# Attention masks on TensorE: two heads' mask matmuls as four quarters of the array, with key tiles taken in swapped pairs by every second head

## The chip, the cores and the metric

The kernel runs on one core of a Trainium2 chip. The metric is the device time of one execution in microseconds (us); lower is better. TensorE multiplies with an array of 128 rows by 128 columns that can also be used in parts (32 or 64 rows or columns each), VectorE and ScalarE read its results from PSUM, GpSimd does some elementwise work, and SyncE issues the DMA transfers.

## The reference

Two decoder layers over 16 batches of 256 tokens of 128 features, with 16 heads of 8 features. Each layer is self-attention, cross-attention to a context of 1601 rows, and a mixture of experts. What matters here is where the scores are masked:

```python
# layer 0: self-attention causal, cross-attention without a mask
scores = einsum('bqhd,bkhd->bhqk', Q, Kp) / sqrt(HD)
if causal: scores = where(tril(ones(Sq, Sk)), scores, -inf)
# layer 1: both masked by integers given for each batch
scores = einsum('bhqd,bhkd->bhqk', q, k) / sqrt(DK)
scores = where(mask[:, None, :, :] == 0, NEG, scores)   # mask (B,256,256) or (B,256,1601)
attn = softmax(scores)
```

A mask is the same for all 16 heads of a batch. Layer 1 follows layer 0 for all batches.

## The kernel before

All work is cut into steps (a `Step` has a kind such as SC or WV), and a planner (`weave`, with its table of costs) puts the steps of one rotation in one order; all engines go through that order. A rotation is one batch of one layer: the cross-attention of batch t, woven with the experts of t-1 and the keys, values and self-attention of t+1, and in layer 1 with the making of masks. There are 32 rotations, 16 of layer 0 and then 16 of layer 1.

Heads go in groups of four. `HP = 32`: head j of a group has its queries and keys on partitions 32j and up, so that its score matmuls use 24 or 25 rows of the array, and different heads' matmuls use different rows. The 1601 keys are 13 tiles of 128 (the last has 65); `key_tiles` gives the two tiles of step i, of seven steps (`KP`).

A beat is one group of matmuls on TensorE: the scores SC of two heads (0 and 1, or 2 and 3) for two key tiles, transposed (keys on partitions, 256 queries for each tile, 512 columns), into two slots of the ring `a`, which has three; with it one or two MC, the maxima's scores of a later group (queries on partitions, 404 keys for each of two heads), into a slot of the ring `d`, which has two. ScalarE reads a slot of `a` and writes the exponentials to `probs_c` (L1082); VectorE reads `d` and reduces it (L918 in layer 0; L926 in layer 1, which adds the mask on the way). WV (L810) multiplies exponentials with values, four heads in four column quarters of the array, and adds them in `sums`. `wait_empty` is the wait for a slot's last reader.

In layer 1 the mask of SC is added by TensorE: a matmul of the 128 x 128 identity in bf16 with the mask (-2^100 or 0, 512 columns) starts the sum in the slot (L773), and the score matmuls (L781) add to it. Self-attention does the same in both layers, with the causal mask in layer 0: MS (maxima, mask at L716, scores L729) and SS (scores, mask at L723, L735). For each head's slot the wait for it and its mask matmul stand together, so the first head's mask is issued before the wait for the second head's slot. NC and NS (L747) are full-array transposes, ES (L886), EF (L874), KC (L842) and VC (L848) full-array matmuls.

Masks come as int32 from memory: ML is the transfer to `mask_words` on SyncE (L1198), MK the cast to bf16 on VectorE (L996); both go in turn through that one buffer. A batch of layer 1 has seven of each: two for self-attention (i of 0 and 1), two for the maxima's masks, and three for the transposed cross mask `mcross_k` (two of six tiles, one for the last 65 keys). At start-up the causal masks are loaded and cast (L1307, L1319).

## Time and profile before

| | |
|---|---|
| Median of 3 runs | 5206.92 us (5200.19 to 5214.99) |
| Span of the profiled execution | 5244.3 us |
| TensorE matmul / weight load busy | 4810.3 / 2757.6 us |
| VectorE / ScalarE / GpSimd busy | 3570.9 / 2804.2 / 654.1 us |
| Chain that ended last | PE 73%, DVE 11%, ACT 6% |
| Mask matmuls L773, busy | 455.4 us |

In the profile PE is TensorE's matmul, PEld its weight load, DVE is VectorE, ACT ScalarE, SPq the queue of SyncE. Times are from the start of the span. A matmul's duration includes the time in which its last results drain, so neighbours overlap; from start to start is what it takes.
### The profile page before, as it was taken

The numbers are of one execution on the slowest core, as the hardware profiler recorded it, in microseconds if no ns is written. First come the engines' busy times: TensorE is split into PE (matmuls) and PEld (weight loads), VectorE is DVE, ScalarE is ACT, GpSimd is POOL, SyncE is SP. The second block draws the span as 40 slices with busy tenths as digits, with TensorE's granted clock in tenths as the row PEclk, the third lists the DMA queues.
The fourth block names the chain that finished last, engine by engine and source line by source line (L and its number), as shares of the span: only waits on it lengthen the run. The fifth ranks groups of instructions, "written<-read, shape, count | busy, mean of one in ns | idle before, by whom it ended". The sixth has DMA issues, their size and how long they took to land.

```text
span 5244.3 us, 103134 instructions
## 1 busy us (share of the span) xinstructions
PE 4810.3 (92%) x40868; PEld 2757.6 (53%) x41312; DVE 3570.9 (68%) x8383; ACT 2804.2 (53%) x5505; POOL 654.1 (12%) x660
## 2 busy tenths in 40 slices
PE   5999999999999988999899999999999999999998
PEld 2454455545555554555545555555555555555556
DVE  4655666566665566666577777777777777777774
ACT  1565566555666565566555455444554444545554
POOL 1101111011111111111111101101101111011100
PEclk7887899878998898899999999999999999999999
DMA  2121122211222222222222332223223223232221
GB/s 61 35 47 40 39 60 56 47 45 35 59 56 60 47 49 42 49 58 74 63 71 69 82 82 67 79 68 87 75 68 81 72 79 82 65 83 70 75 55 63
DMA packets 167993, 327.11 MB, mean 62 GB/s; under 512 B 25656, under 2 KB 76624, under 8 KB 167520
## 3 DMA queue, kind: packets, MB, share of 16 engines
q1 hardware_dynamic: 167520, 320.49, 25.0%
q8 instruction: 335, 5.49, 0.4%
q14 instruction: 138, 1.13, 0.1%
HBM read 237.40 MB, written 4.19 MB: 46 GB/s over the span
## 4 chain that ended last, share of the span: by engine, by line
PE 73%; DVE 11%; ACT 6%; POOL 3%; issue 3%; SPq 2%; DMA 1%; POOLq 0%
PE sums L810 14%; PE a L781 11%; PE d L886 9%; PE a L874 8%; PE a L773 6%; PE d L794 5%; ACT probs_c L1082 4%; PE d L696 3%; PE a L756 2%; SPq L1190 2%; PE a L723 2%; PE d L716 2%; PE d L729 2%; PE d L848 2%; PE d L842 2%
## 5 line engine op out<-in xcount | busy, mean ns | idle before, releaser
L1082 ACT ACTIVATE probs_c<-a 128x512 f32<-128x512 f32 (+1 forms) x3584 | 1833.2, 563 | 1600.9 <-PE a L781 1596.7
L926 DVE CUSTOM_DVE_ANT_0 d<-d,mcross_q 128x404 f32<-128x404 f32 x2048 | 1135.5, 605 | 238.9 <-PE d L794 231.4
L810 PE MATMUL sums<-probs_c,vc 128*32 128x256 f32 x13312 | 1147.0, 419 | 0.2 <-ACT probs_c L1082 0.2
L918 DVE TENSOR_REDUCE chunk_max<-d 128x2 f32<-128x808 f32 x1024 | 994.3, 996 | 166.4 <-PE d L794 161.7
L781 PE MATMUL a<-qc,kc 25*128 25x256 f32 (+1 forms) x6656 | 957.9, 347 | 108.7 <-ACT probs_c L1082 57.0
L794 PE MATMUL d<-kc,qc 24*128 24x404 f32 x4096 | 936.6, 466 | 80.5 <-DVE k_lo L978 22.1
L781 PEld LDWEIGHTS a<-qc,kc 25*128 25x128 f32 (+1 forms) x6656 | 552.2, 190 | 753.4 <-issue 333.9
L874 PE MATMUL a<-xT_e,w_in 128*128 128x256 f32 x2176 | 556.4, 401 | 25.2 <-DMA w_in<-in_experts 20.4
L1063 DVE SCALAR_TENSOR_TENSOR xe<-d,comb,xe 128x128 f32<-128x128 f32 x544 | 165.7, 346 | 571.8 <-PE d L886 571.8
L886 PE MATMUL d<-w_back,hidden 128*128 128x128 f32 x4352 | 548.0, 280 | 1.9 <-DVE chunk_max L926 1.6
L886 PEld LDWEIGHTS d<-w_back,hidden 128*128 128x128 f32 x4352 | 523.9, 194 | 40.8 <-DVE chunk_max L926 15.0
L773 PE MATMUL a<-mcross_k,ident_b 128*128 128x512 bf16 (+1 forms) x1475 | 455.4, 366 | 73.6 <-ACT probs_c L1082 18.2
L794 PEld LDWEIGHTS d<-kc,qc 24*128 24x128 f32 x4096 | 398.4, 192 | 149.7 <-DVE k_lo L978 32.0
L874 PEld LDWEIGHTS a<-xT_e,w_in 128*128 128x128 f32 x2176 | 405.4, 196 | 129.9 <-issue 27.3
L911 DVE TENSOR_REDUCE nm_s<-d 128x4 f32<-128x1024 f32 x256 | 311.8, 1223 | 170.2 <-PE d L729 168.7
L810 PEld LDWEIGHTS sums<-probs_c,vc 128*32 128x32 f32 x13312 | 273.9, 112 | 290.4 <-issue 132.3
L1077 ACT ACTIVATE probs_s<-a 128x512 f32<-128x512 f32 x512 | 277.8, 594 | 261.1 <-PE a L735 261.1
L773 PEld LDWEIGHTS a<-mcross_k,ident_b 128*128 128x128 bf16 (+1 forms) x1792 | 160.1, 99 | 335.5 <-issue 207.2
L926 DVE DVE_READ_ACCUMULATOR2_ANT chunk_max<- 128x1 f32 x2048 | 287.3, 140 | 0.0
L1055 DVE SCALAR_TENSOR_TENSOR hidden<-hidden,a 128x512 f32<-128x512 f32 x288 | 196.4, 686 | 106.6 <-ACT hidden L1105 105.9
L1101 ACT ACTIVATE hidden<-a,b_hid 128x256 f32<-128x256 f32 x512 | 205.8, 476 | 91.6 <-PE a L874 89.7
L1157 POOL TENSOR_TENSOR rstd_s<-mean_var_s,halves 128x2 f32<-128x2 f32 x32 | 22.5, 703 | 1728.5 <-DVE mean_var_s L968 1728.5
(157 smaller groups left out, 4425.5 us busy)
## 6 DMA issues: line engine op xcount, KB each, us to landing
...
kc<-k_hi SPq DMA_DIRECT2D x1024, 50.0 KB
...
kc<-k_lo SPq DMA_DIRECT2D x512, 50.0 KB
...
```

The source lines that it names most:

```text
L773: pe.matmul(T["a"][y.slot][0:y.kn, 0:n * S], T["ident_b"][0:y.kn, 0:y.kn], mask, start=True, stop=False)
L781: last = pe.matmul(T["a"][y.slot][0:y.kn, half * S:(half + 1) * S], T["kc"][rows, y.g, kt * P:kt * P + y.kn], T["qc"][y.p][rows, y.g, :], ...
L794: last = pe.matmul(d[:, h * BANK:h * BANK + CHUNK], T["qc"][y.p][rows, y.g, y.i * P:(y.i + 1) * P], T["kc"][rows, y.g, y.k0:y.k0 + CHUNK], ...
L810: last = pe.matmul(acc[HP * j:HP * j + HP, :], T["vc"][x.p][0:x.kn, v0:v0 + HP], probs_of(T, x)[0:x.kn, j, half:half + S], start=x.j == 0, ...
L874: last = pe.matmul(tile[:, half * S:(half + 1) * S], T["w_in"][load.slot][:, f * P:(f + 1) * P], T["xT_e"][:], start=True, stop=True)
L886: last = pe.matmul(tile[:, qt * D:(qt + 1) * D], hid[:, f, qt * P:(qt + 1) * P], T["w_back"][load.slot][:, f * D:(f + 1) * D], start=f == ...
L911: dve.tensor_reduce(maxima[:, x.j:x.j + 2, :, MROW], tile[:].rearrange("p (h q k) -> p h q k", h=2, q=QT), AX, ALU.max, negate=True).then_ ...
L918: done = dve.tensor_reduce(T["chunk_max"][:, x.g % 2, x.i, x.j:x.j + 2, x.c], tile[:].rearrange("p (h n) -> p h n", h=2)[:, :, 0:CHUNK], A ...
L926: done = dve.tensor_tensor_reduce(some, some, mask, 1.0, -3e38, ALU.add, ALU.max, T["chunk_max"][:, x.g % 2, x.i, x.j + h, x.c:x.c + 1])
L1077: act.activation(T["probs_s"][:, x.j, :], tile[:], ACT.Exp, scale=SCALE).then_inc(M["a_read"], 1)
L1082: act.activation(probs_of(T, x)[0:x.kn, x.j, 0:n], tile[0:x.kn, 0:n], ACT.Exp, scale=SCALE).then_inc(M["a_read"], 1)
L1101: done = act.activation(T["hidden"][x.i % 2][:, f, :], tile[:, half * S:(half + 1) * S], ACT.Gelu, bias=T["b_hid"][:, x.i, f:f + 1])
```

## The change

`half_masks` issues a head's mask as two matmuls of 64 rows by 64 columns by 512 columns of masks: the rows are the lower or upper half of the array, the columns one half each. Two heads of a beat take different row halves, so that their four matmuls lie on four different quarters and on two different banks. Both slots are waited for ahead of the four. In place of two matmuls of 128 x 128 there are four, with four weight loads of 64 x 64.

For this the mask must lie on 64 partitions, four blocks of 64 keys for a pair of key tiles. Of the cross mask, even pairs lie on partitions 0 to 63 and odd pairs on 64 to 127, and nothing is stored twice: every second head (`key_pair`) takes pair i^1 at step i, so that a beat always has one pair of either half. `probs_c` then holds different key tiles for different heads, and WV picks the values accordingly. Self masks and causal masks are stored twice, once on each half. The last 65 keys keep their mask matmul (with both waits ahead). A batch of layer 1 has eight mask steps for seven and thirteen transfers for seven.

```diff
--- before.py
+++ after.py
@@ -40,6 +40,7 @@
 QROWS = 3 * GR
 
 HP = 32
+HALF = P // 2
 ROWS = 3 * HD
 MROW = ROWS
 VW = HD + 1
@@ -264,9 +265,15 @@
     return steps
 
 
+def key_pair(i, j):
+
+    return i ^ (j & 1) if i < KP - 1 else i
+
+
 def key_tiles(x):
 
-    return [2 * x.i, 2 * x.i + 1] if not x.last else [2 * x.i]
+    first = 2 * key_pair(x.i, x.j)
+    return [first, first + 1] if not x.last else [first]
 
 
 class Plan:
@@ -308,7 +315,7 @@
 
     def cross_masks(self, p, batch):
         out = []
-        for i in range(2, 7):
+        for i in range(2, 8):
             out += self.mask(p, i, batch)
             self.at["mcross", p] = out[-1]
         return out
@@ -419,7 +426,7 @@
                 sc.of["mask"] = self.at.get(("mcross", p))
             steps.append(sc)
         if pair:
-            for kt in key_tiles(sc):
+            for kt in range(2 * kp, min(2 * kp + 2, KT)):
                 step = self.make("WV", l=l, p=p, g=g, i=kp, j=kt, kn=kn, last=kt == KT - 1)
                 step.of["sc"] = sc
                 if kt == 0:
@@ -551,7 +558,7 @@
 
     of_kind, rings = {}, {"d": [], "a": []}
     slots = {"d": 2, "a": 3}
-    moved, loaded, groups, tanhs = {}, {}, 0, 0
+    moved, loaded, groups, tanhs, words = {}, {}, 0, 0, 0
     place = {id(x): i for i, x in enumerate(order)}
     for x in order:
         x.n = of_kind.get(x.kind, 0)
@@ -571,6 +578,8 @@
         elif x.kind == "WV":
             x.c = groups
             groups += x.last
+        elif x.kind == "ML":
+            x.c = words = words + mask_parts(x.i)
         elif x.kind == "EF" and x.l == 1:
             x.j, tanhs = tanhs, tanhs + 1
         x.of = {k: v for k, v in x.of.items() if v is not None and id(v) in place}
@@ -671,6 +680,14 @@
         if x.prior.kind == "EF" and x.prior.l == 1:
             pe.wait_ge(M["silu_done"], x.prior.j + 1)
     return x.slot
+
+
+def half_masks(pe, T, out, mask, half):
+
+    rows = slice(half * HALF, (half + 1) * HALF)
+    for n in range(2):
+        pe.matmul(out[n * HALF:(n + 1) * HALF, :], T["ident_b"][rows, rows], mask[rows, n:4:2, :], start=True,
+                  stop=False)
 
 
 def tensor_program(pe, T, M, order):
@@ -711,16 +728,15 @@
                     pe.wait_ge(M["q_made"], nth(y.of["ks"]))
                     if "mself" in y.of:
                         pe.wait_ge(M["masks_made"], nth(y.of["mself"]))
-                mask = (T["mself_q"] if y.l else T["causal_q"])[:].rearrange("p a b -> p (a b)")
                 for h in range(2):
-                    pe.matmul(tile[:, h * BANK:(h + 1) * BANK], T["ident_b"][:], mask, start=True, stop=False)
+                    half_masks(pe, T, tile[:, h * BANK:(h + 1) * BANK], T["mself_q" if y.l else "causal_q"], h)
             for y in scores:
                 if y is not x:
                     wait_empty(pe, M, y)
                 if y.j == 0:
                     pe.wait_ge(M["d_read"], in_ring(y.of["ns"]))
-                mask = (T["mself_k"] if y.l else T["causal_k"])[:].rearrange("p a b -> p (a b)")
-                pe.matmul(T["a"][y.slot][:], T["ident_b"][:], mask, start=True, stop=False)
+            for y in scores:
+                half_masks(pe, T, T["a"][y.slot], T["mself_k" if y.l else "causal_k"], y.j % 2)
             for half in range(2):
                 some = slice(half * P, (half + 1) * P)
                 for y in maxima:
@@ -767,16 +783,19 @@
                     pe.wait_ge(M["d_read"], in_ring(y.of["nc"]))
                 if "mask" in y.of:
                     pe.wait_ge(M["masks_made"], nth(y.of["mask"]))
-                if y.l:
-                    n = len(key_tiles(y))
-                    mask = T["mcross_k"][y.p][0:y.kn, 2 * y.i:2 * y.i + n, :].rearrange("p a b -> p (a b)")
-                    pe.matmul(T["a"][y.slot][0:y.kn, 0:n * S], T["ident_b"][0:y.kn, 0:y.kn], mask, start=True,
-                              stop=False)
+            for y in scores:
+                if y.l and y.last:
+                    pe.matmul(T["a"][y.slot][0:y.kn, 0:S], T["ident_b"][0:y.kn, 0:y.kn],
+                              T["mcross_k"][y.p][0:y.kn, KT - 1, :], start=True, stop=False)
+                elif y.l:
+                    pair = key_pair(y.i, y.j)
+                    half_masks(pe, T, T["a"][y.slot], T["mcross_k"][y.p][:, 4 * (pair // 2):4 * (pair // 2) + 4, :],
+                               pair % 2)
             for half in range(2):
                 for y in scores:
-                    kt = 2 * y.i + half
-                    if kt not in key_tiles(y):
+                    if half >= len(key_tiles(y)):
                         continue
+                    kt = key_tiles(y)[half]
                     rows, ends = head_rows(y.j, ROWS + 1), kt == key_tiles(y)[-1]
                     last = pe.matmul(T["a"][y.slot][0:y.kn, half * S:(half + 1) * S],
                                      T["kc"][rows, y.g, kt * P:kt * P + y.kn], T["qc"][y.p][rows, y.g, :],
@@ -806,7 +825,7 @@
             acc = T["sums"][:, x.g % 2 * S:(x.g % 2 + 1) * S]
             half = x.j % 2 * S
             for j in range(HG):
-                v0 = x.j * VCOLS + (x.g * HG + j) * VW
+                v0 = (2 * key_pair(x.i, j) + x.j % 2) * VCOLS + (x.g * HG + j) * VW
                 last = pe.matmul(acc[HP * j:HP * j + HP, :], T["vc"][x.p][0:x.kn, v0:v0 + HP],
                                  probs_of(T, x)[0:x.kn, j, half:half + S], start=x.j == 0, stop=x.last)
             if x.last:
@@ -992,7 +1011,7 @@
                 "p (a b) -> p a b", a=dest.shape[1])
             if "ss" in x.of:
                 dve.wait_ge(M["a_made"], in_ring(x.of["ss"]))
-            dve.wait_ge(M["words_loaded"], 16 * nth(x.of["words"]))
+            dve.wait_ge(M["words_loaded"], 16 * x.of["words"].c)
             dve.tensor_scalar(dest, view, 0, -BIG, ALU.is_equal, ALU.mult).then_inc(M["masks_made"], 1)
         elif x.kind in ("RT", "R2", "R3"):
             lg, gate, top, idx, idxf = T["lg"], T["gate"], T["top"], T["idx"], T["idxf"]
@@ -1195,7 +1214,9 @@
                 "p (a b) -> p a b", a=dest.shape[1])
             if "mask" in x.of:
                 sp.wait_ge(M["masks_made"], nth(x.of["mask"]))
-            sp.dma_start(view, mask_source(t, x.i, bass.ds(x.batch, 1))).then_inc(M["words_loaded"], 16)
+            for n in range(mask_parts(x.i)):
+                rows = slice(n * HALF, (n + 1) * HALF) if mask_parts(x.i) == 2 else slice(0, dest.shape[0])
+                sp.dma_start(view[rows], mask_source(t, x.i, bass.ds(x.batch, 1), n)).then_inc(M["words_loaded"], 16)
         elif x.kind == "EL":
             if "free" in x.of:
                 sp.wait_ge(M["d_made" if x.j else "a_made"], in_ring(x.of["free"]))
@@ -1211,12 +1232,17 @@
         if moved:
             sp.wait_ge(M["kc_moved", g], 16 * MOVES * len(moved))
     for kind, name in (("LX", "x_loaded"), ("CL", "ctx_loaded"), ("ML", "words_loaded"), ("ST", "stored")):
-        count = sum(x.kind == kind for x in order)
+        count = sum(mask_parts(x.i) if kind == "ML" else 1 for x in order if x.kind == kind)
         if count:
             sp.wait_ge(M[name], 16 * count)
 
 
-MASK_FULL = SK // P
+LAST_KEYS = SK - (KT - 1) * P
+
+
+def mask_parts(i):
+
+    return 1 if i in (2, 3, 7) else 2
 
 
 def mask_tile(T, x):
@@ -1224,19 +1250,20 @@
         return (T["mself_q"], T["mself_k"])[x.i][:]
     if x.i < 4:
         return T["mcross_q"][x.p][:, x.i - 2:x.i - 1, :]
-    if x.i < 6:
-        return T["mcross_k"][x.p][:, (x.i - 4) * 6:(x.i - 3) * 6, :]
-    return T["mcross_k"][x.p][0:SK - MASK_FULL * P, MASK_FULL:MASK_FULL + 1, :]
-
-
-def mask_source(t, i, b):
+    if x.i < 7:
+        return T["mcross_k"][x.p][:, (x.i - 4) * 4:(x.i - 3) * 4, :]
+    return T["mcross_k"][x.p][0:LAST_KEYS, KT - 1:KT, :]
+
+
+def mask_source(t, i, b, part):
     if i < 2:
-        return t[("mself", "mselfT")[i]][b].rearrange("a (q p) k -> (a p) q k", p=P)
+        return t[("mself", "mselfT")[i]][b].rearrange("a (n p) k -> (a p) n k", p=HALF)
     if i < 4:
         return t["mcross"][b, (i - 2) * P:(i - 1) * P, :].rearrange("a p k -> p a k")
-    if i < 6:
-        return t["mcrossT"][b, (i - 4) * 6 * P:(i - 3) * 6 * P, :].rearrange("a (q p) k -> (a p) q k", p=P)
-    return t["mcrossT"][b, MASK_FULL * P:SK, :].rearrange("a p k -> p a k")
+    if i < 7:
+        first = (2 * (i - 4) + part) * 2 * P
+        return t["mcrossT"][b, first:first + 2 * P, :].rearrange("a (n p) k -> (a p) n k", p=HALF)
+    return t["mcrossT"][b, (KT - 1) * P:SK, :].rearrange("a p k -> p a k")
 
 
 def build(nc, t, out):
@@ -1258,7 +1285,7 @@
 
     T = {
         "ident": sb("ident", [P, P]), "ident_b": sb("ident_b", [P, P], BF16), "iota": sb("iota", [P, E0]),
-        "causal_q": sb("causal_q", [P, QT, S], BF16), "causal_k": sb("causal_k", [P, QT, S], BF16),
+        "causal_q": sb("causal_q", [P, 2 * QT, S], BF16), "causal_k": sb("causal_k", [P, 2 * QT, S], BF16),
         "w_pad": sb("w_pad", [P, 2, 3, NG, P]), "b_pad": sb("b_pad", [P, 2, 3, NG]),
         "low_rows": sb("low_rows", [P, 2]), "w_key": sb("w_key", [P, 2, D]), "w_val": sb("w_val", [P, 2, 2, VCOLS]),
         "w_out": sb("w_out", [P, 2, 2, D]), "b_k": sb("b_k", [P, 2]), "b_val": sb("b_val", [P, 2, 2, VCOLS]),
@@ -1269,7 +1296,7 @@
         "vc": pair("vc", [P, KT * VCOLS + VPAD]), "vs": sb("vs", [P, QT * VCOLS + VPAD]),
         "qs": sb("qs", [P, NG, S], F32R), "ks": sb("ks", [P, NG, S], F32R), "qc": pair("qc", [P, NG, S], F32R),
         "q_sum": pair("q_sum", [P, NG, S]), "q_high": sb("q_high", [P, NG, S], F32R),
-        "mself_q": sb("mself_q", [P, QT, S], BF16), "mself_k": sb("mself_k", [P, QT, S], BF16),
+        "mself_q": sb("mself_q", [P, 2 * QT, S], BF16), "mself_k": sb("mself_k", [P, 2 * QT, S], BF16),
         "mcross_q": pair("mcross_q", [P, QT, SK], BF16), "mcross_k": pair("mcross_k", [P, KT, S], BF16),
         "probs_c": pair("probs_c", [P, HG, BANK]), "probs_s": sb("probs_s", [P, HG, BANK]),
         "hidden": pair("hidden", [P, NF, S]), "w_in": pair("w_in", [P, FF]),
@@ -1304,7 +1331,9 @@
     for name in loads:
         sp.dma_start(T[name][:], t[name]).then_inc(set_up, 16)
     for n, name in enumerate(("causal_q", "causal_k")):
-        sp.dma_start(T["probs_c"][n][:, 0:QT, 0:S], t[name]).then_inc(set_up, 16)
+        for half in range(4):
+            rows, of = slice(half // 2 * HALF, (half // 2 + 1) * HALF), slice(half % 2 * HALF, (half % 2 + 1) * HALF)
+            sp.dma_start(T["probs_c"][n][rows, half % 2:2 * QT:2, 0:S], t[name][of]).then_inc(set_up, 16)
     for l in range(2):
         sp.dma_start(w_split[l], t["w_split"][:, l]).then_inc(set_up, 16)
     for tile in (T["b_pad"], T["low_rows"], T["w_pad"], T["nm_s"], T["nm_c"]):
@@ -1315,9 +1344,9 @@
     dve.memset(T["q_sum"][0][:], 1.0)
     dve.memset(T["k_hi"][:].bitcast(F32), 1.0).then_inc(cleared, 1)
     dve.wait_ge(cleared, 1)
-    dve.wait_ge(set_up, 16 * (len(loads) + 4))
-    dve.tensor_copy(T["causal_q"][:], T["probs_c"][0][:, 0:QT, 0:S])
-    dve.tensor_copy(T["causal_k"][:], T["probs_c"][1][:, 0:QT, 0:S])
+    dve.wait_ge(set_up, 16 * (len(loads) + 10))
+    dve.tensor_copy(T["causal_q"][:], T["probs_c"][0][:, 0:2 * QT, 0:S])
+    dve.tensor_copy(T["causal_k"][:], T["probs_c"][1][:, 0:2 * QT, 0:S])
     dve.tensor_copy(T["ident_b"][:], T["ident"][:])
     for part in range(3):
         for l, n in ((0, 0), (0, 1), (0, 2), (1, 0), (1, 1), (1, 2)):
```

## Rows read from the trace of the kernel before

**Rows 1.** The page: busy us of each engine, and the granted clock in 40 slices.

```profile
PE 4810.3 (92%) x40868; PEld 2757.6 (53%) x41312; DVE 3570.9 (68%) x8383; ACT 2804.2 (53%) x5505; POOL 654.1 (12%) x660
...
PEclk7887899878998898899999999999999999999999
```

**Rows 2.** Windows by stretch: us, busy time (count) of each engine, PEclk, DMA share, GB/s.

```profile
404.30:2633.10 2228.80, 2012.01 (x17085) 1168.88 (x17164) 1381.58 (x2240) 1315.89 (x2577) 324.03 (x323) 0.88 0.22 52
404.30:570.70 166.40, 152.48 (x1224) 86.91 (x1226) 98.18 (x156) 94.03 (x185) 23.11 (x23) 0.82 0.21 48
1850.60:1999.00 148.40, 133.32 (x1228) 79.05 (x1230) 97.98 (x156) 93.99 (x185) 23.11 (x23) 0.95 0.23 53
2799.90:5067.60 2267.70, 2163.47 (x18680) 1228.08 (x18984) 1739.54 (x5137) 1136.24 (x2241) 248.47 (x252) 1.00 0.29 75
3286.10:3448.10 162.00, 154.61 (x1338) 87.74 (x1358) 124.39 (x368) 81.16 (x160) 17.69 (x18) 1.00 0.30 76
```

**Rows 3.** Windows before and in a fall, and the timeline where it rose.

```profile
584.30:591.10 6.80, 5.24 (x47) 2.03 (x40) 5.24 (x5) 3.20 (x6) 2.20 (x1) 1.00 0.02 4
591.10:621.80 30.70, 28.92 (x162) 13.80 (x161) 16.53 (x27) 9.66 (x20) 3.74 (x5) 0.50 0.09 12
...
619.87 2.68 PE L848 MATMUL d<-w_val,ctxT 128*128 128x144 f32 x12
```

**Rows 4.** The mask lines: duration min/median/max, first and last start, forms.

```profile
L773 PEld LDWEIGHTS a<-mcross_k,ident_b x1792: 94/97/181, 2633.1 to 5195.1; 128*128 128x128 bf16 x171, 65*65 65x65 bf16 x29
L773 PE MATMUL a<-mcross_k,ident_b x1475: 270/379/634, 2633.3 to 5195.2; 128*128 128x512 bf16 x152, 65*65 65x256 bf16 x33
...
L716 PEld LDWEIGHTS d<-causal_q,ident_b x256: 95/99/119, 43.5 to 2377.8; 128*128 128x128 bf16 x128
...
L723 PEld LDWEIGHTS a<-causal_k,ident_b x256: 95/98/152, 51.7 to 2387.6; 128*128 128x128 bf16 x128
```

**Rows 5.** TensorE timeline of two beats in layer 1, masks behind sums: start, us.

```profile
2750.94 0.60 PE L773 MATMUL a<-mcross_k,ident_b 128*128 128x512 bf16 x2
2751.47 0.38 PE L781 MATMUL a<-qc,kc 25*128 25x256 f32 x2
...
2751.69 0.28 PE L781 MATMUL a<-qc,kc 25*128 25x256 f32 x2
2751.90 0.64 PE L810 MATMUL sums<-probs_c,vc 128*32 128x256 f32 x8
2752.47 0.60 PE L773 MATMUL a<-mcross_k,ident_b 128*128 128x512 bf16 x2
...
2753.01 0.38 PE L781 MATMUL a<-qc,kc 25*128 25x256 f32 x2
```

**Rows 6.** ScalarE timeline in the same beats: the first head's exponential.

```profile
2752.01 0.60 ACT L1082 ACTIVATE probs_c<-a 128x512 f32<-128x512 f32 x1 [0.45 <-PE a L781]
```

**Rows 7.** TensorE timeline, masks behind full-array transposes.

```profile
4002.82 0.44 PE L747 MATMUL d<-ident,nm_s 128*128 128x128 f32 x2
4003.09 0.59 PE L773 MATMUL a<-mcross_k,ident_b 128*128 128x512 bf16 x2
4003.62 0.39 PE L781 MATMUL a<-qc,kc 25*128 25x256 f32 x2
```

**Rows 8.** TensorE timeline of layer 0 at full clock, scores of two beats.

```profile
529.68 0.38 PE L781 MATMUL a<-qc,kc 25*128 25x256 f32 x2 [0.25 <-ACT probs_c L1082]
...
530.96 0.38 PE L781 MATMUL a<-qc,kc 25*128 25x256 f32 x2 [0.21 <-ACT probs_c L1082]
```

**Rows 9.** Casts of masks, SyncE's longest wait, start-up transfers of a causal mask.

```profile
L996 DVE TENSOR_SCALAR mcross_k<-mask_words x48: 277/952/956, 2527.9 to 5012.5; 128x1536 bf16<-128x1536 int32 x32, 65x256 bf16<-65x256 int32 x16
...
L996 DVE TENSOR_SCALAR mself_q<-mask_words x16: 416/420/422, 2444.4 to 4880.1; 128x512 bf16<-128x512 int32 x16
...
SPq L1185 <- PE a L781: 1621.8, 124, 69.9
...
6.71 0.68 SPq L1307 DMA_DIRECT2D probs_c<-in_causal_q  x1
```

## The prediction

> **What bounds the kernel now.** I read the page's busy line first: TensorE is busy for 92% of the span, VectorE 68%, ScalarE 53% [rows 1]. The clock line under it says that the two halves differ: layer 0 (the first 2.6 ms) runs at 0.7 to 0.9 of full clock, layer 1 at full clock [rows 1]. The windows view by stretch gives both stages [rows 2]. In layer 1 TensorE is busy 2163 of 2268 us, 95%, at clock 1.00; some of the other 5% are mask matmuls whose records are missing, since 1792 loads at L773 stand against 1475 matmul records [rows 4]. So layer 1 is bound by TensorE, with VectorE at 77% and ScalarE at 50%. In layer 0 TensorE is busy 90% at clock 0.88. A rotation of the loop (one batch of one layer: 56 beats of two heads' scores) takes 162.0 us in layer 1 (2268 us are 14 of them) and 148 to 166 us in layer 0.
>
> The layer-0 rotations hold the same work, so their difference is a price list for the clock. The level is 1.0 or 0.5, hence the time at 0.5 is twice what the mean lacks of 1. One rotation has 0.82 over 166.4 us, 60 us at the low level (1.2 GHz); another has 0.95 over 148.4 us, 15 us [rows 2]. 18 us more time for 45 us more at the low level: **0.40 us lost per us at 1.2 GHz**. Over layer 0 the low level holds 24% of the time (2 x 0.12).
>
> What was the engine doing when the clock fell? In the 6.8 us before 591.1 it ran scores, maxima and sums, small tiles of the array with waits for VectorE and ScalarE in between, 5.24 us busy; then the level was 0.50 for 30.7 us, though TensorE counts as 94% busy in them [rows 3]. It rose at 621.8, after 12 full-array matmuls of L848 [rows 3]. A beat of layer 0 has no mask; a beat of layer 1 has two full-array mask matmuls, and there the clock doesn't fall at all between 2800 and 5067 us.
>
> **What the change removes: mask streaming.** Counted by weight loads [rows 4]: 1792 at L773, of which 256 are the 65-key tails that stay as they are, so 1536 or 768 pairs; 512 at L716 and 512 at L723 (256 in each layer), 256 pairs each. That is 1280 pairs. A pair behind the sums of L810 takes 0.54 us up to the scores (2750.94 to 2751.47) [rows 5]: two streams of 512 columns at 2.4 GHz, 0.213 each, and 0.11 for loads and for the array's handover from one tiling to the next. As four quarters in one stream of 512 columns it would be 0.32 us plus whatever four loads of 64 columns cost. No row has a 64 x 64 tile. The nearest: four column quarters at L810 (eight matmuls in two sets) take 0.57 us for two sets of 0.213, so 0.03 a set over; the 128-column loads of L781 cost 0.11 between first and second half (0.22 apart, 256 columns of 0.107) [rows 5]. I take 0.04 to 0.06 for loads and issue, nearer to L810 since it is a column-tiled set too: 0.36 to 0.38 us. Saved: 0.17 us a pair, at most 0.216. That the four run side by side I take from rows: column quarters do (L810) and row quarters do (two heads' L781 in 0.38 us, together) [rows 5]. Ceiling for the kernel: 1280 x 0.216 = 276 us, 5%.
>
> **What takes part of it back.** (a) *The second slot.* Today the first mask starts when the first head's slot is free, and the second head's wait lies behind that stream. Now both waits stand ahead of all four matmuls. In the second beat shown [rows 5] the first mask is at 2752.47, but the second slot is read out only when ScalarE ends at 2752.01 + 0.60 = 2752.61 [rows 6], 0.04 more until TensorE sees it. Today that costs nothing, since the second stream isn't due before 2752.70; scores at 2753.01. After: 2752.65 + 0.37 = 2753.02. Gain nil. Of the 470 cross pairs behind sums or another tiled step, some 330 are like that (counted down the timeline; one is shown, [rows 5, 6]), the other 140 gain 0.17: 24 us. (b) *A handover that wasn't there.* 281 cross pairs follow a full-array step (NC, NS, ES, EF). The masks can follow two transposes with no gap [rows 7] (two transposes 4002.82 to 4003.09, then two masks of 0.27 each until 4003.62). As quarters they need a handover on that side too, 0.10 us as between masks and scores. 0.17 - 0.10 = 0.07 x 281 = 20 us. (c) *Self-attention.* The maxima's masks (256 pairs) have no such slot wait within the pair: 0.17 at full clock and some 0.3 at half, less a handover for some: 45 us. The score masks behind them mostly wait for ScalarE's slot: 256 x 0.03 = 8 us. Sum of a to c: 97 us. (d) In the tails the first head's 256-column mask now waits for the second slot: 128 x 0.03 = 4 us back. The bounds are 60 us, if loads cost 0.11 as at L781, and 276 us. I take 93 us.
>
> **What it adds.** VectorE: the self mask casts grow from 512 to 1024 elements, between 0.42 and 0.95 us, so 0.69 [rows 9]: 32 x 0.27 = 9 us; the cross casts become 3 of 1024 for 2 of 1536 elements, 16 x 0.17 = 3 us. VectorE has 23% idle in layer 1 and the masks are made a rotation ahead; cost 0, and 12 us if that cover were gone. SyncE: 13 transfers for 7 in a batch and 512 KB more, six more issues of 0.4 to 0.7 us [rows 9]. Queued behind them are key moves and expert loads, but the queue itself stands waiting for TensorE 1622 us at L1185 alone [rows 9]. Cost 0, at most 16 x 6 x 0.4 = 38 us. Start-up: eight transfers for two ahead of the w_split load at up to 0.68 each now [rows 9], and nothing starts until these are in: 3 us. The swapped pairs change which key tile a head takes and nothing of count or size: 0. The planner has one more mask step in each layer-1 batch and may order a rotation a little differently: 0, within 10 us each way. Together 5 us.
>
> **The clock.** This is the term that decides. Half of the full-array streaming of masks goes, and where the slot binds no time is saved for it, so the same stretch merely holds less array work: it comes to look like layer 0's beat of scores and sums, 1.28 us with a wait for ScalarE in it [rows 8]. Layer 1 now spends 0% at the low level with whole masks and layer 0 24% without cross masks [rows 2]; with half the masks I put layer 1 between, at 8%: 185 us. Once down, it stays down until a run of expert or value matmuls, as there [rows 3]. Layer 0 loses half of its self masks in just the stretches where it is warm or returns to it; I take one more fall per rotation, 12 us x 15.5 = 185 us. Bounds: 0, and 24% of layer 1 (540 us) with 250 in layer 0. Taken: 370 us at 0.40, **148 us lost**; bounds 0 and 316.
>
> **Sum.** -93 + 5 + 148 = +60 us. The profiled execution spans 5244.3 us and would be 5304; it is 0.7% above the median of the timed runs, so against 5206.9 I forecast 5267, rounded to **5270 us**.
>
> [...]
>
> **Rivals.**
> 1. *The clock doesn't move.* The mask savings stand alone: 5207 - 93 + 5 = 5119 us (5080 to 5160). For it: layer 1's clock stands at 1.00 over 14 rotations, through their thin moments too [rows 2]. Against: layer 0 falls in each rotation. It decides if layer 1 shows under 2% at the low level and layer 0 no more than now. Chance 0.20.
> 2. *The clock costs about half of that*, 180 us more at the low level: 5207 - 88 + 72 = 5191, with 5175 to 5225 around it. Chance 0.16.
> 3. *Full saving*: neither slot nor handover takes anything and the loads hide, 5207 - 276 + 5 = 4936 us, up to 5040 with part of it. Against: [rows 5, 6]. Chance 0.04.
> 4. *The quarters don't all overlap*: two sets of 0.213 for a pair, one per row half or column half. Then a pair takes what it takes now plus 0.03 to 0.06 of loads, plus the handovers: 1280 x 0.05 + 281 x 0.10 = 92 us, 5300 us, and 5450 with the clock. Against: [rows 5]. Chance 0.08.
> 5. *The forecast*: slot-bound and clock lost, 5225 to 5350. Chance 0.50. What is left, 0.02, is outside all this (transfers late, another order).
>
> **How the numbers follow.** A measurement of this kernel can tell about 0.3% (16 us) from no change, so "same" is 5191 to 5223. Faster: rivals 1 and 3 and 0.06 of rival 2, 0.30. Same: half of rival 2 and a little of the rest, 0.08. Slower: the forecast, rival 4 and what is left, 0.62. The range from 5110 to 5360 holds the forecast's body, rival 2, most of rival 1 and the near part of rival 4; outside are rival 3, the low end of 1 and the clock's upper bound, about 0.18. The likeliest case's own range is 5225 to 5350.
>
> **What would show it.** At the mask line, L773's successor, four matmuls start within 0.03 us, and scores begin 0.36 to 0.38 us after the first load: right for the pair. If 0.54 or more, rival 4. In the SC-WV pattern the beat stays at 1.53 to 1.57 us, with mask matmuls waiting for ScalarE: right for the slot; 1.36 would be rival 3. In the clock line layer 1 must show levels under 1.00 in most rotations and layer 0 a mean below 0.88; rotations of 162 us become some 158 where the clock holds and 165 or more where it fell. Wrong would be a clock line as before, or a layer 1 at 0.99 with rotations under 158 us.

## The result, and the profile after

The changed kernel takes 5478.3 us (median of 4 runs, 5473.1 to 5522.1) against 5211.0 us; the ratio is 1.054 [1.050, 1.058]. It is slower by 267 us, where I had forecast 5270 us with a range up to 5360. The direction was right; the size is four times the forecast one, and outside the range. Ratios set a kernel against the runs of before timed beside it and leave out runs over 1.5% above the fastest of their kernel, so they needn't be the quotient of the medians shown.

The page of the changed kernel, its busy line and its clock line (to set beside [rows 1]):

```profile
PE 4922.3 (90%) x43872; PEld 2830.2 (52%) x43872; DVE 3596.2 (66%) x8399; ACT 2806.0 (51%) x5505; POOL 653.5 (12%) x660
...
PEclk7788879898888888777899899989999899998999
```

TensorE is busy 112 us more, with half the mask columns to stream. Not all of that is real: 444 mask records are missing in the trace of before (40868 matmuls for 41312 loads) and none here, up to some 95 us at 0.21 each. The clock line shows the rest of the story: layer 1, all nines before, has an eight in every fourth or fifth slice.

The windows view of the changed kernel: 14 rotations of layer 0, 14 of layer 1, and two single rotations of layer 1 (columns as in [rows 2]):

```profile
261.80:2497.30 2235.50, 2028.05 (x17616) 1186.88 (x17620) 1375.31 (x2172) 1315.95 (x2576) 323.85 (x322) 0.85 0.22 50
2850.60:5298.30 2447.70, 2238.64 (x20780) 1270.97 (x20781) 1762.59 (x5151) 1137.61 (x2241) 247.17 (x252) 0.92 0.30 73
4078.60:4250.70 172.10, 156.62 (x1488) 89.25 (x1492) 125.85 (x369) 81.30 (x161) 17.64 (x18) 0.94 0.31 75
3020.60:3201.70 181.10, 167.50 (x1490) 93.80 (x1492) 126.40 (x369) 81.26 (x160) 17.66 (x18) 0.87 0.30 71
```

The windows view of the kernel before, from the same beats to the same beats:

```profile
245.30:2468.90 2223.60, 2016.34 (x17084) 1170.87 (x17168) 1374.46 (x2172) 1316.16 (x2576) 323.57 (x322) 0.87 0.22 50
2801.00:5068.70 2267.70, 2163.31 (x18679) 1228.10 (x18992) 1739.54 (x5137) 1136.22 (x2241) 248.47 (x252) 1.00 0.29 75
```

The cut at the start of layer 1 lies 49.6 us later (2850.6 for 2801.0), the 14 rotations of layer 1 take 180.0 us more, and what is left behind them is equal: together the 230 us by which the two profiled executions differ (5474.1 and 5244.3). Of the 49.6, 16.5 lie ahead of layer 0's cut (7.5 of them start-up), 11.9 in its 14 rotations and 21.2 between the two cuts.

The two single rotations do the same work and differ by 9.0 us. Their clock means are 0.94 and 0.87; by the clock's own records, which have the levels 1.00 and 0.50 and no other, they spent 20.5 and 47.8 us at the low level, so a us at it costs 0.33 us there, and a rotation that stayed at full clock would take 172.1 - 0.33 x 20.5 = 165.3 us, against 162.0 before [rows 2]. So layer 1 lost twice: 3.3 us a rotation with no clock in it, and 9.6 us on average by the clock. In the tables below "base" is this intercept, a straight line through 14 rotations, and "low" the sum of their time at the low level.

The mask matmuls themselves did what was promised. Their groups on the page of the changed kernel:

```profile
L689 PE MATMUL a<-mcross_k,ident_b 64*64 64x512 bf16 x3072 | 330.3, 416 | 120.1 <-ACT probs_c L1101 47.3
...
L689 PEld LDWEIGHTS a<-mcross_k,ident_b 64*64 64x64 bf16 x3072 | 99.7, 105 | 415.5 <-ACT probs_c L1101 205.3
```

The timeline of TensorE in the changed kernel, two beats of layer 1 (L689 masks, L800 scores, L829 sums):

```profile
4609.56 0.41 PE L689 MATMUL a<-mcross_k,ident_b 64*64 64x512 bf16 x4
4609.90 0.38 PE L800 MATMUL a<-qc,kc 25*128 25x256 f32 x2
...
4610.13 0.28 PE L800 MATMUL a<-qc,kc 25*128 25x256 f32 x2
4610.33 0.64 PE L829 MATMUL sums<-probs_c,vc 128*32 128x256 f32 x8
4611.18 0.41 PE L689 MATMUL a<-mcross_k,ident_b 64*64 64x512 bf16 x4 [0.21 <-ACT probs_c L1101]
4611.52 0.39 PE L800 MATMUL a<-qc,kc 25*128 25x256 f32 x2
```

And ScalarE's first exponential between them, from the same timeline:

```profile
4610.44 0.60 ACT L1101 ACTIVATE probs_c<-a 128x512 f32<-128x512 f32 x1 [2.23 <-PE a L800]
```

Four matmuls start as one group (x4) and the scores follow 0.34 us later (4609.56 to 4609.90), against 0.53 [rows 5]. The 64-column loads, for which the prediction had no row, take 105 ns each, against 97 for those of 128 columns [rows 4], and overlap: the last three of the second beat's start within 6 ns (4611.181 to 4611.187). But look at the second beat. The sums start at 4610.33 and take 0.57 [rows 5]; the masks start not at 4610.90 but at 4611.18, "0.21 <-ACT". ScalarE's first exponential ends at 4610.44 + 0.60 = 4611.04, and the masks start 0.14 us behind it. The beat takes 1.62 us from masks to masks, where it took 1.53 [rows 5]. It is no odd one: over the beats of scores and sums at full clock in layer 1 the median is 1.62 us (298 beats) for 1.55 before (333).

### The profile page after: what moved, and what is told of

Read it like the earlier page. It is cut to its first block, busy times and chain, and to the rows that moved or that the text cites. A ratio compares the mean times of both kernels' runs of the same rounds, so it can differ in the third digit from the quotient of the medians.

```text
span 5474.1 us, 109599 instructions
## 1 busy us (share of the span) xinstructions
PE 4922.3 (90%) x43872; PEld 2830.2 (52%) x43872; DVE 3596.2 (66%) x8399; ACT 2806.0 (51%) x5505; POOL 653.5 (12%) x660
## 4 chain that ended last, share of the span: by engine, by line
PE 71%; DVE 10%; ACT 9%; SPq 3%; issue 3%; POOL 2%; DMA 2%; POOLq 0%
PE sums L829 12%; PE a L800 11%; PE d L905 9%; PE a L893 8%; PE a L689 7%; ACT probs_c L1101 6%; PE d L813 5%; PE d L713 3%; SPq L1209 3%; PE a L772 3%; PE d L745 2%; PE d L867 2%; ACT probs_s L1096 2%; PE d L861 2%; DVE chunk_max L937 2%
## 5 line engine op out<-in xcount | busy, mean ns | idle before, releaser
L829 PE MATMUL sums<-probs_c,vc 128*32 128x256 f32 x13312 | 1206.0, 438 | 0.2 <-ACT probs_c L1101 0.2
L813 PE MATMUL d<-kc,qc 24*128 24x404 f32 x4096 | 981.4, 482 | 113.9 <-DVE k_lo L997 50.7
L800 PE MATMUL a<-qc,kc 25*128 25x256 f32 (+1 forms) x6656 | 989.6, 358 | 104.3 <-ACT probs_c L1101 57.4
L800 PEld LDWEIGHTS a<-qc,kc 25*128 25x128 f32 (+1 forms) x6656 | 573.3, 197 | 690.3 <-ACT probs_c L1101 320.8
L813 PEld LDWEIGHTS d<-kc,qc 24*128 24x128 f32 x4096 | 415.6, 199 | 184.9 <-DVE k_lo L997 59.7
L689 PE MATMUL a<-mcross_k,ident_b 64*64 64x512 bf16 x3072 | 330.3, 416 | 120.1 <-ACT probs_c L1101 47.3
L829 PEld LDWEIGHTS sums<-probs_c,vc 128*32 128x32 f32 x13312 | 278.4, 114 | 305.6 <-issue 151.8
L930 DVE TENSOR_REDUCE nm_s<-d 128x4 f32<-128x1024 f32 x256 | 313.3, 1224 | 167.4 <-PE d L745 165.3
L689 PEld LDWEIGHTS a<-mcross_k,ident_b 64*64 64x64 bf16 x3072 | 99.7, 105 | 415.5 <-ACT probs_c L1101 205.3
```

Of the source, the lines that this page charges most:

```text
L689: pe.matmul(out[n * HALF:(n + 1) * HALF, :], T["ident_b"][rows, rows], mask[rows, n:4:2, :], start=True, stop=False)
L800: last = pe.matmul(T["a"][y.slot][0:y.kn, half * S:(half + 1) * S], T["kc"][rows, y.g, kt * P:kt * P + y.kn], T["qc"][y.p][rows, y.g, :], ...
L813: last = pe.matmul(d[:, h * BANK:h * BANK + CHUNK], T["qc"][y.p][rows, y.g, y.i * P:(y.i + 1) * P], T["kc"][rows, y.g, y.k0:y.k0 + CHUNK], ...
L829: last = pe.matmul(acc[HP * j:HP * j + HP, :], T["vc"][x.p][0:x.kn, v0:v0 + HP], probs_of(T, x)[0:x.kn, j, half:half + S], start=x.j == 0, ...
L930: dve.tensor_reduce(maxima[:, x.j:x.j + 2, :, MROW], tile[:].rearrange("p (h q k) -> p h q k", h=2, q=QT), AX, ALU.max, negate=True).then_ ...
```

## Experiments

The prediction's theory is that masks with half the array work cost layer 1 its clock (Theory A in most of the expectations). The rival that the windows suggest is the order (Theory B): the planner was given an eighth pair of mask steps, and layer 1's base rose where it should have fallen. A third candidate is the wait for both heads' slots. Doing one part alone, undoing one part, and giving the array work back tell them apart. No run tries the swapped key pairs by themselves, nor the thirteen transfers and the wider self-mask casts; every kernel with quarters has them all.

All are timed against the kernel before. Bases and low times are of one profiled execution of each kernel, over 14 rotations of each layer.

| kernel | median us | ratio to before | layer 0: base, low | layer 1: base, low |
|---|---|---|---|---|
| before | 5211 to 5229 | 1 | 144.4, 561 | 162.0, 0 |
| after | 5478 | 1.054 [1.050, 1.058] | 145.2, 651 | 165.2, 410 |
| e1_order | 5583 | 1.071 [1.064, 1.077] | 143.8, 630 | 170.5, 468 |
| e2_eight | 5342 | 1.023 [1.019, 1.028] | 144.2, 540 | 166.7, 181 |
| e3_waits | 5458 | 1.047 [1.041, 1.052] | 143.3, 682 | 161.4, 457 |
| e4_twice | 5585 | 1.069 [1.064, 1.075] | 146.0, 504 | 175.1, 287 |
| e5_fill | 5126 | 0.980 [0.974, 0.986] | 147.8, 113 | 162.0, 0 |
| e6_old_order | 5378 | 1.023 [1.012, 1.034] | 143.4, 685 | 160.8, 236 |
| e7_order_waits | 5305 | 1.014 [1.008, 1.021] | 143.5, 699 | 159.3, 171 |
| e8_eight_old | 5226 | 1.000 [0.997, 1.004] | 143.7, 418 | 161.9, 0 |
| e9_twice_old | 5333 | 1.023 [1.017, 1.028] | 145.6, 410 | 168.5, 7 |
| e10_no_mask | 5150 | 0.987 [0.983, 0.991] | 143.9, 527 | 150.2, 273 |
| e11_fill_half | 5219 | 1.000 [0.996, 1.004] | 149.4, 396 (see below) | 162.0, 0 |
| e12_fill_256 | 5145 | 0.985 [0.981, 0.989] | 145.1, 229 | 162.0, 0 |

Layer 0's low time isn't the same in every execution of the same code: 561 us in before, 418 in e8_eight_old, whose layer 0 is identical. One kernel against one says little there; groups of kernels do (below).

**The order of steps.** Comparing the orders of steps of the two kernels shows what the eighth pair did: layer 0 is unchanged up to its last rotation (39 steps there), but of the 346 steps of a layer-1 rotation that aren't mask steps, 129 stand at another place (39 have to be moved to make one order of the other). e2_eight does only this to the kernel before (with the matching cut in `mask_source`), and has exactly the order of the changed kernel:

```diff
-        for i in range(2, 7):
+        for i in range(2, 8):
...
-        return T["mcross_k"][x.p][:, (x.i - 4) * 6:(x.i - 3) * 6, :]
+        return T["mcross_k"][x.p][:, (x.i - 4) * 4:(x.i - 3) * 4, :]
```

> The kernel before, with its three transposed mask pieces made four of which three hold four tiles, so that the planner gives the order of the changed kernel; full-array mask matmuls as before. Theory A: within 1% of before, 5190 to 5250 us, layer 1 at clock 1.00 and 162 to 164 us a rotation. Theory B (order): 5260 to 5350 us.

It lost 2.3%, with full-array masks. The windows view of e2_eight, layer 1:

```profile
2790.00:5177.30 2387.30, 2288.38 (x18988) 1253.77 (x18992) 1751.50 (x5151) 1137.58 (x2241) 247.23 (x252) 0.96 0.28 71
```

One line of its waits view for TensorE in that window (us in total, times, longest):

```profile
PE d L794 <- DVE k_lo L978: 32.1, 28, 1.9
```

The same line of the kernel before:

```profile
PE d L794 <- DVE k_lo L978: 5.8, 14, 0.4
```

The base rose by 4.7 us a rotation and the clock fell for 13 us in each. The lines are the waits of the maxima's scores for a slot of `d` from which VectorE makes `k_lo`, the low-order part of the keys; they are over five times what they were, and 2 us of the 4.7. In the new order VectorE also waits for a mask's transfer, 19.4 us in 14 times (`DVE mcross_k L996 <- DMA mask_words<-in_mcrossT: 19.4, 14, 2.1` in its waits view), which it doesn't in the old. Which of the moved steps cost the rest isn't settled. e8_eight_old has the eight steps too, but keeps the old order, with the extra cast and transfer put between the transfer (ML) and the cast (MK) of the second piece. Against e2_eight its edit is:

```diff
-        for i in range(2, 8):
+        for i in range(2, 7):
...
-    return weave(plan.model, LENGTH[t // B], (0, 1, plan.attention(t)), *side)
+    return with_third(weave(plan.model, LENGTH[t // B], (0, 1, plan.attention(t)), *side))
...
+    between = Step("MK", p=load.p, i=5)
+    between.of = {"words": load}
+    again = Step("ML", p=load.p, i=6, batch=load.batch)
+    again.of = {"mask": between}
...
+    middle = (a + b) // 2 + 1
+    return steps[:middle] + [between, again] + steps[middle:]
```

> The kernel before with eight mask steps (as e2_eight), but in its own old order, the extra pair in the middle of the second piece's gap. If e2_eight lost by the order: within 0.5% of before, 5195 to 5245 us, layer 1 at clock 1.00 and 162 us a rotation. If it lost by the eighth cast and transfer themselves: 5300 to 5350 us, as e2_eight.

1.000 [0.997, 1.004], layer 1 at 161.9 us a rotation and full clock. So the eighth cast and its transfer are free, and the order is what costs. (Its transfers are whole ones, eight in all, and its self masks have the old width.)

e1_order and e6_old_order give the changed kernel the old order. They differ in where the extra pair stands. In e1_order it stands directly ahead of the last piece's transfer:

```diff
-        for i in range(2, 8):
+        for i in (2, 3, 4, 5, 7):
...
+        if x.kind == "ML" and x.i == 7:
+            load = Step("ML", p=x.p, i=6, batch=x.batch)
+            load.of = dict(x.of)
+            cast = Step("MK", p=x.p, i=6)
+            cast.of = {"words": load}
+            x.of["mask"] = cast
+            out += [load, cast]
```

In e6_old_order it stands in the middle of the second piece's gap; the edit is that of e8_eight_old, made to the changed kernel:

```diff
-        for i in range(2, 8):
+        for i in range(2, 7):
...
-    return weave(plan.model, LENGTH[t // B], (0, 1, plan.attention(t)), *side)
+    return with_third(weave(plan.model, LENGTH[t // B], (0, 1, plan.attention(t)), *side))
```

> The changed kernel, but with the planner seeing seven mask steps as before; the eighth pair of transfer and cast is put in behind its back, so all other steps have the order of before. Theory A (clock and slot wait make the loss): the order matters little, 5430 to 5490 us, layer-1 rotations at 170 to 181 us as in the changed kernel. Theory B (the new order of layer 1 makes the loss): 5300 to 5380 us, and the time of a rotation that stays at full clock falls from 165 to 162 us or less.

> The changed kernel with the order of the kernel before for all steps other than mask steps; this time the third transposed piece's transfer and cast lie in the middle of the 35 us between transfer and cast of the second, so that VectorE doesn't stand waiting for a transfer (which spoilt e1_order, 194 us of waiting). Theory B (order and quarters add up, 117 us for the order by e2_eight): 5340 to 5400 us, layer-1 rotations that stay at full clock at 160 to 163 us. Theory A (the order matters only with whole masks, the quarters' clock and slot cost is the same in any order): 5440 to 5500 us.

e1_order came out slower than the changed kernel and outside both ranges, for a reason of its own: VectorE, in order, stood waiting for the transfer just issued. A line of its waits view for VectorE (us in total, times, longest):

```profile
DVE mcross_k L1030 <- DMA mask_words<-in_mcrossT: 194.3, 16, 12.3
```

That is 12 us a rotation, and it says nothing on the order; for this transfer a cast that is not to wait must stand some 12 us behind (longest wait 12.3). e6_old_order has none of it: 5378 us, 100 us under the changed kernel by medians, and 105 us under it in layer 1 of the profiled executions (2342.5 for 2447.7, window below). Its runs spread from 5314 to 5420, more than others, at mean clocks from 0.906 to 0.879, and the two ratios (1.054 and 1.023) are some 160 us apart, so the size is known to some tens of us only. e2_eight put the order at 117 with whole masks, so order and quarters roughly add up. The base falls from 165.2 to 160.8, below before's 162.0, and the low time from 410 to 236 us.

**The joint wait.** e3_waits and e7_order_waits issue each head's quarters directly behind that head's wait, in the new and the old order:

```diff
-            for y in scores:
-                half_masks(pe, T, T["a"][y.slot], T["mself_k" if y.l else "causal_k"], y.j % 2)
+                half_masks(pe, T, T["a"][y.slot], T["mself_k" if y.l else "causal_k"], y.j % 2)
...
-            for y in scores:
                 if y.l and y.last:
```

> The changed kernel with each head's wait for its slot directly ahead of its own two quarter matmuls, as before the change, so that the first head's quarters don't wait for the second slot. Theory A (the joint wait costs 0.06 us in each beat bound by the ring): 5400 to 5450 us, the beat of scores and sums falls from 1.59 us to about 1.53. If the wait is only moved, since the second head's quarters still take 0.34 us after it: 5470 to 5490 us and 1.59 us.

> e6_old_order with each head's wait directly ahead of its own quarters. If the joint wait costs as in e3_waits, 20 us under e6_old_order. If the quarters save time as forecast before the change was seen (93 us without the clock), the base of a layer-1 rotation at full clock goes to 157 to 160 us, and what is above it is the clock's: 0.33 to 0.4 us for each us at the low level.

The windows view of e3_waits, layer 1:

```profile
2852.80:5289.30 2436.50, 2336.31 (x20780) 1313.18 (x20782) 1763.08 (x5151) 1138.10 (x2241) 247.22 (x252) 0.91 0.31 73
```

The same of e6_old_order:

```profile
2856.60:5199.10 2342.50, 2174.44 (x20780) 1245.20 (x20784) 1751.72 (x5151) 1135.29 (x2241) 246.33 (x252) 0.95 0.32 76
```

The same of e7_order_waits:

```profile
2851.90:5138.80 2286.90, 2214.34 (x20780) 1262.61 (x20784) 1743.31 (x5151) 1136.06 (x2241) 248.35 (x252) 0.96 0.33 78
```

And of e7_order_waits a single rotation that stayed at full clock:

```profile
2851.90:3011.10 159.20, 153.48 (x1488) 87.85 (x1492) 124.51 (x369) 81.13 (x160) 17.75 (x18) 1.00 0.35 81
```

In the old order the separate waits give 56 us in layer 1 (2342.5 to 2286.9), 73 by medians (5378 to 5305) and 44 by the two ratios; base 160.8 to 159.3, low time 236 to 171. The intervals of the ratios overlap, and e6_old_order alone spreads by more than this, so the times by themselves don't prove it; the beats do. Their median, 1.62 us in the changed kernel and in e6_old_order, is 1.52 in e3_waits and in e7_order_waits, as expected of e3_waits if the joint wait is what costs. The total of e3_waits lies between its two ranges: in the new order the base falls by 3.8 us a rotation, 53 us in 14, but layer 1 takes only 11 us less and the whole 20, since the low time rose from 410 to 457 us and each us of it cost more (0.39 for 0.33). The clock took back most of what the wait gave. e7_order_waits is the change at its best, and shows the gain of quarters with all that comes with them: at full clock a rotation takes 159.2 us for 162.0, 2.8 us or 1.7%. Over 16 rotations that would be 45 us. It is still 1.4% slower than before, because 171 us at the low level cost 57 us in these 14 rotations alone (2286.9 less 14 x 159.3), and because of layer 0.

**Layer 0.** It has no cross masks, and its order is the same in all these kernels; only its self masks differ. The five kernels with one set of quarters show 630 to 699 us at the low level (mean 669), the four with whole masks (before, e2, e8, e10) 418 to 561 (mean 512), the two with the quarters issued twice 504 and 410. The ranges of the first two groups don't touch, and twice the quarters bring the low time back into the range of whole masks. And the beat at which layer 1's windows start comes at 2850.6 to 2860.9 us in the five and at 2760.5 to 2801.0 in the four: 50 us or more apart. Some 6 of them are start-up, whose end, the first exponential, comes at 121.0 to 124.3 us in the five and at 115.0 to 117.0 in the four. The bases are alike, 143.3 to 145.2 with quarters and 143.7 to 144.4 without.

**The clock.** e4_twice and e9_twice_old issue each set of quarters twice, in the new order and (with separate waits) in the old:

```diff
+    for again in range(2):
         for n in range(2):
             pe.matmul(out[n * HALF:(n + 1) * HALF, :], T["ident_b"][rows, rows], mask[rows, n:4:2, :],
-                      start=True, stop=False)
+                      start=again == 0, stop=False)
```

> The changed kernel with every set of quarter mask matmuls issued twice (the mask added twice, which masks as well): the array gets as much mask work as before the change, in as much time. Theory A (the clock fell because array work went away): layer 1 back at clock 0.98 to 1.00, layer 0 above 0.87, in all 5300 to 5420 us, so faster than the changed kernel though it does more. Theory C (the clock has to do with the tiling or with something else): the clock stays where it is and 1280 more sets of 0.21 us come on top, 5650 to 5750 us.

> e7_order_waits with each set of quarter masks issued twice, so that a beat of layer 1 streams as much mask through as much of the array as the kernel before, in the same order of steps. Theory A (the clock goes with the array work per time): layer 1 back at clock 1.00, layer 0 as before (0.87 to 0.92), rotations of layer 1 between 162 and 168 us, 5220 to 5320 us in all. Theory C (tiling, not work, moves the clock): layer 1 keeps 10 us and more at the low level in most rotations, over 5400 us.

The windows view of e9_twice_old, layer 1:

```profile
2796.10:5158.00 2361.90, 2331.60 (x24364) 1280.09 (x24368) 1751.37 (x5151) 1136.55 (x2240) 248.16 (x252) 1.00 0.31 75
```

e9_twice_old is clear on the clock: with the array work of before and the order of before, layer 1 is back at clock 1.00, 7 us at the low level in place of 171. The tiling doesn't hold the clock down; missing work does, and whether that is time of streaming or part of the array these two can't tell (e11_fill_half and e12_fill_256 below do). Its time, 5333 us, is above Theory A's range, since the second set costs 9 us a rotation (168.5 for 159.3). e4_twice was to be faster than the changed kernel and isn't: its low time fell from 410 to 287 us only, because the new order makes falls of its own (181 us in e2_eight), and the second set cost 10 us a rotation. The clock theory was half right there; what it missed is the order, which I had not yet put in.

e10_no_mask takes the mask matmuls of layer-1 cross-attention away altogether (in the scores only, so the softmax there is unmasked):

```diff
-                if y.l:
-                    n = len(key_tiles(y))
-                    mask = T["mcross_k"][y.p][0:y.kn, 2 * y.i:2 * y.i + n, :].rearrange("p a b -> p (a b)")
-                    pe.matmul(T["a"][y.slot][0:y.kn, 0:n * S], T["ident_b"][0:y.kn, 0:y.kn], mask, start=True,
-                              stop=False)
```

> The kernel before without TensorE's mask matmuls in layer-1 cross-attention: the softmax there is taken over unmasked scores, and the maxima and self-attention are masked as ever. It takes away 768 pairs at once. Theory A: layer 1 leaves clock 1.00 and looks like layer 0, 25 to 60 us at the low level a rotation; at full clock a rotation would be 145 to 155 us, and at 0.35 us per us at the low level it is 160 to 170 us: no gain or a loss, 5180 to 5330 us. Theory C (masks don't carry the clock): 148 to 155 us a rotation and 4950 to 5080 us in all.

The windows view of e10_no_mask, layer 1:

```profile
2785.30:5004.90 2219.60, 2009.43 (x17422) 1181.08 (x17424) 1717.03 (x5137) 1133.07 (x2241) 245.27 (x252) 0.94 0.30 77
```

The base falls by 11.8 us a rotation, 165 us in 14; but the layer's 14 rotations take 2219.5 us for 2267.7, a gain of 48. The clock took back 70%. Its 273 us at the low level (20 a rotation, below the 25 I expected) cost 0.43 us for each us. In all it took 5150 us, between the two ranges and nearer to Theory A's: a gain where that theory had none or a loss.

**Work added for the clock.** If missing array work costs the clock, layer 0 should gain by more of it. e5_fill adds to the kernel before one full-array matmul of zeros in each beat of layer-0 cross-attention, in the first head's slot, ahead of the wait for the second's:

```diff
+    return x.l == 0 and x.j % 2 == 0 and not x.last
...
+                if filled(y):
+                    pe.matmul(T["a"][y.slot][0:y.kn, 0:len(key_tiles(y)) * S], T["ident_b"][0:y.kn, 0:y.kn],
+                              T["zeros"][0:y.kn, 0:len(key_tiles(y)) * S], start=True, stop=False)
```

e11_fill_half makes two quarters of it (64 rows, 2 x 64 columns), and e12_fill_256 halves its columns:

```diff
+                    for n in range(2):
+                        some = slice(n * P // 2, (n + 1) * P // 2)
+                        pe.matmul(T["a"][y.slot][some, :], T["ident_b"][0:P // 2, 0:P // 2], T["zeros"][0:P // 2, :],
...
+                    pe.matmul(T["a"][y.slot][:, 0:S], T["ident_b"][:], T["zeros"][:, 0:S], start=True, stop=False)
```

> The kernel before with one full-array matmul of zeros more in each layer-0 beat of cross-attention, for the first head only, added into its scores and issued ahead of the wait for the second head's slot (it changes no result). Theory A (the clock falls where TensorE does little full-array work): layer 0 goes from a mean clock of 0.88 to above 0.96, and at 0.36 us per us gained at full clock its 2500 us shrink by 100 to 200 us: 5030 to 5130 us in all, though 768 matmuls of 0.21 us were added. Theory C (full-array work has nothing to do with it): layer 0 stays at 0.86 to 0.90, 5210 to 5370 us.

> e5_fill with its matmul of zeros as two quarters side by side (64 rows, 2 x 64 columns of the array, 512 columns streamed) in place of the full array: the same streaming time for half the array. Theory A (the part of the array counts): layer 0's mean clock lies between before and e5_fill, 0.90 to 0.95, and the time between 5140 and 5220 us. Theory D (only the time counts in which TensorE streams): as e5_fill, clock 0.96 to 0.98 in layer 0, 5110 to 5145 us.

> e5_fill with its matmul of zeros over 256 columns in place of 512 (the first key tile's half only): half the added work. Theory A (added full-array work buys clock, and costs what it takes beside the wait for ScalarE): layer 0's mean clock between those of before and e5_fill, 0.91 to 0.96; a rotation that stays at full clock costs 145 to 147 us instead of 147.8; in all 5120 to 5180 us, between the two kernels. If the wait hides the whole fill anyway, nothing is won by halving it and the time is above e5_fill's.

The windows view of e5_fill, 14 rotations of layer 0:

```profile
241.30:2356.60 2115.30, 1956.68 (x17574) 1131.96 (x17837) 1384.05 (x2173) 1316.52 (x2576) 323.51 (x322) 0.97 0.23 53
```

The same of e12_fill_256:

```profile
243.60:2365.30 2121.70, 2003.62 (x17840) 1160.12 (x17844) 1374.97 (x2173) 1316.54 (x2577) 324.31 (x322) 0.95 0.23 53
```

e5_fill is the fastest kernel of the study, 5126 us and 0.980 [0.974, 0.986] of before, though it does 768 useless matmuls more. Layer 0's clock rises from 0.87 to 0.97, its 14 rotations fall from 2223.6 to 2115.3 us; at full clock a rotation costs 3.4 us more. Per matmul that is 0.07 us for 0.21 us of streaming: the wait for ScalarE [rows 8] hides the rest. e12_fill_256 costs only 0.7 us a rotation, but keeps 229 us at the low level for 113. The profiled execution of e11_fill_half, at 5268 us, is the longest of its ten, so I read its clock from the timed runs: a mean over the whole kernel of 0.962 (median; 0.950 to 0.973), against 0.937 in before, 0.964 in e12_fill_256 and 0.979 in e5_fill. e11_fill_half streams as long as e5_fill through half the array, e12_fill_256 half as long through all of it, and both lift the clock alike; if the time of streaming alone counted, e11_fill_half would be at e5_fill's 0.979. That is Theory A's clock and not Theory D's. In time e11_fill_half gains nothing, 1.000 [0.996, 1.004], at the upper end of Theory A's range. By its profiled execution a rotation at full clock takes 149.4 us, 5.0 more than before and 1.6 more than with e5_fill's one full matmul of the same length; that is 80 us in 16 rotations, and by the mean clocks (0.962 for 0.937) some 260 us less at the low level give back about as much, an estimate at 0.36 us each.

## Why the prediction was wrong

**The order of steps is the term that failed first.** I wrote "the planner has one more mask step in each layer-1 batch and may order a rotation a little differently: 0, within 10 us each way". It was 117 us by e2_eight, and 100 by medians, 105 in layer 1 or 160 by the ratios by e6_old_order, the largest single part by each. Its cost is of both kinds: by e2_eight 4.7 us a rotation at full clock and 181 us at the low level. I could have built the two orders' difference from the planner's text: its queue of cross masks is spread over a fixed part of the rotation, and one more entry moves all entries, which the greedy choice then carries to everything else. The kernel before was at 162.0 us, rotation after rotation, with TensorE at least 95% busy: a reshuffle of such an order had little to gain and much to lose.

**The second slot** was the right mechanism with the wrong size. I put 0.04 us from the slot's read-out to the load, because a load that was next anyway started so: the second mask's, at 2752.654, where the exponential ends at 2752.61 [rows 6]. With TensorE idle and waiting, the masks start 0.14 us behind the end of the exponential, and the beat is 1.62, not my 1.53 to 1.57. I counted "gain nil" for 330 pairs; each lost up to 0.09 us. The joint wait costs 56 us in layer 1 by e6_old_order against e7_order_waits. With it, in the old order, a rotation at full clock takes 160.8 us for 162.0: 19 us saved in 16 rotations, where the forecast had some 67 for layer 1 (24, 20 and half of the self masks, less the tails). The delay could have been read beforehand: layer 0's scores wait for ScalarE [rows 8], and the exponential ahead of the first of these rows, in the timeline of ScalarE of the kernel before, ends at 529.54 us, 0.14 ahead of the scores' 529.68, and in all 337 waits of L781 for ScalarE in that trace the distance is the same:

```profile
528.94 0.60 ACT L1082 ACTIVATE probs_c<-a 128x512 f32<-128x512 f32 x1 [0.30 <-PE a L781]
```

The changed kernel's waits view for TensorE in layer 1 (us in total, times, longest) shows it:

```profile
PE a L689 <- ACT probs_c L1101: 64.0, 240, 0.8
PE a L689 <- ACT probs_s L1096: 38.2, 82, 0.8
```

The first of these in the same view of the kernel before:

```profile
PE a L773 <- ACT probs_c L1082: 15.9, 100, 0.2
```

**The quarter set** was right: 0.34 us from start to scores, against 0.36 to 0.38 forecast; the four overlap, and rival 4 is out. The ceiling of 276 us was never near. At full clock and with the slot waits separate, e7_order_waits saves 2.8 us a rotation in layer 1, and layer 0's base is that of whole masks within 0.3 us (means 143.8 and 144.1): 16 x 2.8 + 16 x 0.3, some 50 us for the 93 forecast. Half of the 45 and 8 us forecast for self masks belongs to layer 0, and hardly any of that half came.

**The clock** was right in sign and mechanism and too small. I took 185 us more at the low level in layer 1 and 185 in layer 0. Layer 1 shows 410 in 14 rotations, 17% where I had put 8%; 181 appear in e2_eight by the order alone, and in the old order 236 in e6_old_order, with the joint wait, and 171 in e7_order_waits without it, so for the change without its order my 185 for layer 1 was of the right size. The price in layer 1 was 0.30 to 0.39 us per us in the changed kernel and its variants (0.33 in itself), not 0.40. Layer 0 was somewhat too small: by the groups of kernels above 669 against 512 us in 14 rotations, 157 more, and from the start of the span to layer 1's first rotation means of 886 against 645, 241 more for my 185. Over the whole execution the changed kernel is at the low level for 1328 us and the kernel before for 720 (twice what their mean clocks, 0.879 and 0.931, lack of 1): 608 more for my 370. So of rival 1, "the clock doesn't move", nothing holds, and TensorE's busy share doesn't tell the clock: layer 1 is 96% busy in e3_waits with 457 us at the low level and 93% busy in e6_old_order with 236. (The 95% of before isn't to be compared with these: 313 of its mask records are missing there.) Where I had put a rotation that holds the clock at 158 us, it is 165.3.

**Casts and transfers** at 0: right for the eighth cast and its transfer (e8_eight_old). The wider self casts and the split transfers were in no run by themselves; e7_order_waits, which has them all, stays under before's 162.0 us a rotation at full clock, and VectorE waits for a mask's transfer once in it, for 1.8 us. Start-up, up to the first exponential, cost 7.5 us for my 3 (124.3 for 116.8).

The sum, from the profiled executions: of the 180 us in layer 1, 105 are the order, 56 the joint wait and 19 the quarters as such (2286.9 for 2267.7: some 38 saved in 14 rotations, 57 lost to the clock). These are differences of single executions, taken in this sequence; in the new order the joint wait is worth 11 us in layer 1. The 50 ahead of layer 1 are start-up (7.5) and, by the groups of kernels above, mostly layer 0's clock. Together 230; the medians' 267 is larger because the profiled execution of before was 0.6% above its own median. With the old order and separate waits the time is e7_order_waits' 5305, inside my range; with the order alone undone it is e6_old_order's 5378, still above it.
